# 16-wide attentions: where the third unit's score pieces for the row maxima begin

## The reference

```python
def _L0_attn_a_ref(x, Wq, Wk, Wv, Wo):
    ...
    Q = split_heads(x @ Wq.T)
    K = split_heads(x @ Wk.T)
    V = split_heads(x @ Wv.T)
    scores = jnp.einsum('bhqd,bhkd->bhqk', Q, K) / jnp.sqrt(jnp.float32(HEAD_DIM))
    causal = jnp.tril(jnp.ones((s, s), dtype=bool))
    scores = jnp.where(causal, scores, jnp.float32(-jnp.inf))
    attn = jax.nn.softmax(scores, axis=-1)
    out = jnp.einsum('bhqk,bhkd->bhqd', attn, V)
```

## Time and profile before

| | us |
|---|---|
| median of the three runs | 2844.2 |
| the profiled execution's own time | 2843.15 |
| its span in the trace | 2841.4 |
| PE busy | 2663.5 (94%) |
| DVE busy | 1740.5 (61%) |
| ACT busy | 1423.9 (50%) |
| POOL busy | 726.5 (26%) |

### The profile page before, as it was taken

How to read it: one execution, slowest core, us unless ns; L and a number is a source line. 1 busy time by engine, 2 the same in 40 slices (tenths; PEclk the granted TensorE clock), 3 DMA queues, 4 the chain that set the end, 5 groups by cost and what they waited for, 6 DMA issues and landing times. The chain is left out here.

```text
span 2841.4 us, 46262 instructions
## 1 busy us (share of the span) xinstructions
PE 2663.5 (94%) x16809; PEld 1962.9 (69%) x16809; DVE 1740.5 (61%) x3727; ACT 1423.9 (50%) x2943; POOL 726.5 (26%) x861
## 2 busy tenths in 40 slices
PE   7989998999999998899999999998999999989879
PEld 4444465654486887688788888877888888754545
DVE  7758645678446766776576666653343332477597
ACT  3645633536544433433455555455556553337476
POOL 3012002040001432333211110024545541130185
PEclk9999999999999999999999999999999999999999
DMA  3022010021110531332100000010000000120031
GB/s 99 26 56 65 2 52 29 1 57 36 34 34 29 143 109 39 112 114 89 30 22 19 16 22 18 1 34 23 12 19 16 12 31 14 41 71 22 13 103 56
DMA packets 73852, 122.31 MB, mean 43 GB/s; under 512 B 16286, under 2 KB 47360, under 8 KB 73488
## 3 DMA queue, kind: packets, MB, share of 16 engines
q1 hardware_dynamic: 72028, 118.05, 13.9%
q10 hardware_dynamic: 1600, 1.31, 0.3%
HBM read 92.21 MB, written 1.54 MB: 33 GB/s over the span
## 5 line engine op out<-in xcount | busy, mean ns | idle before, releaser
L130 PE MATMUL psum<-L1f_hT_part,L1f_wide 128*128 128x512 f32 x1104 | 269.2, 393 | 11.5 <-DVE L1f_inner L2926 9.0
L236 POOL TENSOR_TENSOR scale<-scale,powers 128x1 f32<-128x1 f32 (+1 forms) x98 | 57.4, 586 | 857.8 <-DVE scale L217 857.8
L130 PEld LDWEIGHTS psum<-L1f_hT_part,L1f_wide 128*128 128x128 f32 x1104 | 201.3, 188 | 56.9 <-DVE L1f_inner L2926 14.1
L2734 POOL TENSOR_TENSOR L1f_inner<-L1f_inner,L1f_weight 128x512 f32<-128x512 f32 x96 | 144.8, 1517 | 264.0 <-DVE L1f_inner L2926 179.3
L1281 ACT ACTIVATE L0f_weights<-psum 128x512 f32<-128x512 f32 (+2 forms) x320 | 156.9, 567 | 92.6 <-PE psum L1097 71.9
L1817 ACT ACTIVATE L2b_weights<-psum,L2b_inverse 128x512 f32<-128x512 f32 x192 | 109.9, 581 | 151.2 <-PE psum L130 151.2
L2865 ACT ACTIVATE L1f_gate<-psum 128x512 f32<-128x512 f32 x96 | 57.4, 598 | 213.2 <-PE psum L130 181.9
L130 PE MATMUL psum<-L1f_down,L1f_inner_part 128*128 128x256 f32 x1152 | 154.3, 285 | 7.8 <-DVE L1f_down L2937 4.2
L130 PEld LDWEIGHTS psum<-L1f_down,L1f_inner_part 128*128 128x128 f32 x1152 | 150.2, 193 | 15.1 <-DVE L1f_inner_part L2942 9.3
L1749 PE MATMUL psum<-L2b_v,L2b_weights 128*128 128x129 f32 x1152 | 145.6, 276 | 13.1 <-DVE L2b_rows L1901 10.2
L1749 PEld LDWEIGHTS psum<-L2b_v,L2b_weights 128*128 128x128 f32 x1152 | 140.5, 191 | 22.0 <-issue 12.6
(11 more groups left out here) (585 smaller groups left out, 6677.6 us busy)
## 6 DMA issues: line engine op xcount, KB each, us to landing
L1f_w<-in_L1f_w SPq DMA_DIRECT2D x32, 384.0 KB, 3.5
L1f_weight<-combine SPq DMA_DIRECT2D x32, 384.0 KB, 4.4
L1f_weight<-combine SPq DMA_DIRECT2D x32, 256.0 KB, 4.6
scan_spread_b<-bc SPq DMA_DIRECT2D x16, 512.0 KB, 3.6
L0f_qs<-L0f_part SPq DMA_DIRECT2D x96, 64.0 KB, 2.6
experts_early<-in_L1f_w SPq DMA_DIRECT2D x16, 384.0 KB, 3.7
L0f_ks<-L0f_part SPq DMA_DIRECT2D x86, 64.0 KB, 2.6
L1f_weight<-combine SPq DMA_DIRECT2D x32, 128.0 KB, 4.0
```

The source lines that it names most:

```text
L130: last = nc.tensor.matmul(to, stationary, moving, start=start and n == 0, stop=stop and n == len(pairs) - 1, skip_group_check=skip)
L2734: nc.gpsimd.tensor_tensor(inner[u % INNER][:], inner[u % INNER][:], weight[n % SPREAD][:, half * HALF:(half + 1) * HALF], ALU.mult).then_i ...
```

## The change

One expression in `narrow_order`: for the third unit alone (`u == 2`) the stretch of its pieces begins at slot 0 (two slots before the first unit's due slot, held at 0) and no longer at slot 3. It ends at slot 11 as before. So its 27 pieces lie in 11 slots and no longer in 8.

```diff
     for u in range(1, len(QUAD_UNITS)):
         todo = [m for m in pieces[FIRST_PIECE[u]:FIRST_PIECE[u + 1]] if m not in order]
-        a, b = max(due[u - 1] - 2, 0), due[u] - 2
+        a, b = max(due[u - 1 - (u == 2)] - 2, 0), due[u] - 2
         for n, m in enumerate(todo):
             at_slot.setdefault(a + n * (b - a) // len(todo), []).append(m)
         at_slot.setdefault(due[u], []).append(f"t{u}")
```

## The result

| | before | after |
|---|---|---|
| median of five runs (us) | 2844.2 | 2861.7 |
| lowest to highest | 2840.9 to 2848.0 | 2858.8 to 2869.0 |
| the profiled execution's own time | 2843.15 | 2868.97 |
| ratio of the times, 95% interval | | 1.0073 (1.0060 to 1.0087) |

The change makes the kernel 17.5 us slower by the medians. 2861 us was predicted, 2850 to 2867. The profiled execution is the slowest of the five; its trace shows the order of the steps, but its total, 25.8 us over the one of before, isn't the median's. The falls of the clock differ between executions of one kernel: over the five of the change the mean granted clock lies between 0.977 (the profiled one) and 0.982 (the median).

What follows compares the result with a forecast made beforehand. DVE bounds PE before slot 16, and SP's in-order queue of 24 copies sets slot 16. Delay of 12.9 us plus 3.7 for the clock gives 16.6, added to the 2844.2 median: 2861 us, range 2850 to 2867.

Steps and rivals of the forecast that it cites:

- The chain over SP: Late copy of second unit's maxima delays its place_max, 24 queued SP copies, third place_max and slot 16: 12.9 us.
- Rival C: Early pieces fill DVE waits, so the second unit's copy keeps its time: not slower, 2844 or 2842.3 us; chance 0.10.
- Rival A: Slot 16 is delayed but the clock stays full or falls only within the pause: 12.9 us, 2857; chance 0.20.
- D: PE recovers at most 1.9 us behind slot 16 through fewer bank waits: 2859; counted within the forecast's 0.60.
- Rival B: SP's 24 copies, started later, issue faster and return 7.4 us, leaving 5.5: 2850 us; chance 0.10.
- The size of the delay: Slot 16 later by 3.6 us in L0a and first L0f, 3.25 in second L0f, 2.46 in L3a; sum 12.9.
- Slot 8: Second place_max lands at 59.2 us in L0a, slot 8 comes near 60.1: landing hidden with some 0.9 us to spare.
- The clock: PE's pause before slot 16 lowers the clock, costing 1.22 us in three stages of four: 3.7 us.
- a sign that I had named wrongly: At slot 16 PE would wait for the DMA 4 to 5 us in L0a, 3 to 4 in L0f.
- the third unit's own copy: DVE's copy of the third unit's maxima stays where it was or comes up to 0.53 us earlier; costed at nothing.
- That behind slot 16 the lists are the same: After slot 16 lists are unchanged and PE is full, so nothing is given back there.
- the sign that I had named: From slot 16 to the stage's end the length should be as before within 1.5 us.

Runs made afterwards that it cites:

- e2: Kernel before the change, with only the second unit's turn moved down the list, six pieces later; no piece moved against a slot: 2861.2 us, ratio 1.0070.
- e4: Kernel before the change, with six more copies (30 instead of 24) issued by SP between the second and third place_max: 2870.5 us, ratio 1.0099.
- e1: Changed kernel with only the second unit's turn moved back up the list, six pieces sooner; the early pieces stay: 2846.5 us, ratio 1.0017.
- e3: Changed kernel with six of SP's 24 copies issued ahead of the second unit's place_max; other engines' lists untouched: 2848.2 us, ratio 1.0024.
- e5: Changed kernel with the fourth ring bank opened one piece later, turning the bank rotation by one; lists unchanged: 2860.7 us, ratio 1.0065.
- e7: Kernel of e4 with 17 matmuls of zeros keeping PE busy in the pause ahead of slot 16: 2859.9 us, ratio 1.0055.
- e9: Kernel of e3 with the bank rotation of e5 and five matmuls of zeros where PE waits for the second unit's fold: 2845.7 us, ratio 1.0009.
- e8: Kernel before the change, with six of SP's 24 copies issued ahead of the second unit's place_max: 2838.9 us, ratio 0.9990.
- e6: Changed kernel with piece m21 put back directly behind m20, folding the second unit's maxima sooner; the turn stays late: 2866.8 us, ratio 1.0082.

## Why the prediction was right

**The chain over SP** was right in each link from the second copy to slot 16. Both directions are shown: a late turn alone makes slot 16 late by 12.0 us in all (e2), extra copies alone do so too (e4, 14.9), and in the changed kernel either an early turn (e1) or six copies out of the way (e3) takes most of the loss back. Rival C, no delay, fell with the copy at 56.57 us (its last time should have been 2842.5 us and not 2842.3). Rival A, no cost of the clock, fell with the half clock behind slot 16 in L0a and L3a. Of D, PE taking the delay in, nothing is to be seen: with the ring set right, e5 takes 87.32 and 87.30 us behind slot 16 in L0f, before took 87.34 and 87.31. Rival B, shorter copies, fell with 17.8, 16.1, 16.4 and 16.4 us from the second place_max to the third, where before it was 17.6, 16.6, 16.4 and 16.7.

**The size of the delay.** I had 3.6, 3.6, 3.25 and 2.46 us for slot 16, 12.9 in all. Measured were 3.78, 3.35, 3.87 and 2.15, 13.15 in all. The second copy itself came 3.59 us later in L0a, 3.85 and 3.88 in the L0f stages and 3.50 in L3a, counted from the first one. L3a's slack of 1.14 us was no property of the list but the fall at 2552.5 us of this one trace.

**Slot 8** did not wait for its DMA, as costed. But it came at 62.36 us in L0a, not near 60.1; in e3, where the clock held, it is at 60.45.

**The clock.** The term of 3.7 us was near in sum and not in its parts. I had put 1.22 us in three stages of four behind slot 16. The profile has it in two, 1.6 us in L0a (20.25 against 18.63 to the fourth copy) and 2.8 in L3a (21.57 against 18.79), together 4.4. It fell in the two stages where PE waited longest for the DMA (2.63 and 3.66 us) and not in the two L0f (1.55 and 1.33). A fall of 6.8 us costs 1.9 to 2.8 us, as e4 and e7 show, and the 1.22 from L3a in the earlier trace rows was a fall half as long.

**What I missed** is the fall between slots 4 and 6. It also answers a sign that I had named wrongly: I expected waits of 4 to 5 us at slot 16 in L0a and 3 to 4 in L0f, and they were 2.63, 1.55 and 1.33. PE was late there itself, by the half clock from 53.3 us on. In the change this cost is hidden, since SP is later still. The prediction had left the third unit's own copy where it was, or 0.53 us earlier; behind the half clock it came 2.3, 2.0 and 2.6 us later in L0a and L0f, counted from the first copy (29.41, 32.80 and 33.39 us against 27.08, 30.82 and 30.83). As soon as SP is out of the way this is the next thing in line. In e3's trace the four stages are 3.2 us over before, with such a fall in two of them, and e9 has 6.7 us less there, 2.3 of it the ring's. By the medians, though, e3 is 6.5 us over before and e9 3.1, so the typical run gains only half of what these two traces show.

**That behind slot 16 the lists are the same** was the reason for a term of nothing besides the clock there, and this step failed, by 0.55 us a stage, 2.2 in all. The lists are the same but the ring isn't: moving m21 behind m24 changes which piece had the fourth turn's bank last, m77 and no longer m76, and the turn waits for it (e5). By the sign that I had named, the end of a stage within 1.5 us of before after slot 16, L0a and L3a broke it, for the most part through the clock.

**Luck.** The stages of the profiled execution lost 19.9 us: 13.15 ahead of slot 16, 4.4 by the clock and 2.2 by the ring behind it. The prediction had 16.6, and lacked the ring. That 2861 met the median of 2861.7 so closely is luck: the median execution has a higher granted clock than the profiled one (0.982 against 0.977), and no trace shows how its 17.5 us are made up. The mechanism and the 13 us ahead of slot 16 are not luck.

## What to carry to other kernels

Before moving work forward in one engine's list, look for what it overtakes, and follow that through every in-order queue, the DMA issuer's too: a small DMA that is 3.6 us late holds back 24 that have nothing to do with it, and whoever waits for the next small one pays. A list entry that others hang on (a turn, a fold) wants its own place, apart from the bulk that is spread around it. And where a queue has idle time before a wait, put some of the copies from behind the wait into it, as many as fit: in e8 six held the second place_max up by 1.6 us, which cost nothing only because slot 8 didn't yet need it.

## What the hardware showed

- The clock fell after no long pause. At 53.3 us in L0a PE had waited 1.03 us once and some 0.2 us at several pieces, and was busy 2.06 of the 3.30 us before; in the kernel before it was busy 2.79 of the same 3.30 and kept its clock. It isn't settled by that alone: with the same 2.06 of 3.30 us e3 kept it in L0a. In the stretch from 9 to 16 us behind the first copy the clock fell in 15 of the 20 stages of the five kernels with early pieces and no zeros (the change, e1, e3, e5, e6), in none of the 24 stages of the six with the pieces where they were, and in none of the four of e9, with the zeros. What decides it from one stage to the next is open.
- The fall then lasted 3.4 or 6.8 us of the trace and cost 1.6 to 2.8 us in a stretch where PE is full. The Trainium skill (TensorE: Matmul & The Clock Gate, Part 1) ties the fall to an idle array, and in one kernel to short idle stretches between groups of matmuls. The falls between slots 4 and 6 are of the second kind: the array had worked six tenths of the time, and its longest wait was 1.03 us in L0a.
- SP's issue of a copy of 64 KB takes 0.59 us in the median whether it is early or late; 24 of them take 15.2 to 17.0 us, before the change and after it.
